# Transposing the normed attention output by DMA instead of by TensorE, in a two-layer graph network

## The reference, cut to what matters

```python
# x: (1250, 1024) float32; layer 0
qkv = x @ W_qkv                                   # 16 heads of 64
attn = relu(q @ k.T * SCALE)
out = attn @ v                                    # (1250, 1024)
normed = (out - mu) / sqrt(var + EPS) * gamma + beta
y_mix = normed @ W_out + b_out                    # "the output product"
h = x_normed @ W_gnn.T + b                        # the graph product, (1250, 1024)
y_gnn = A_hat @ h                                 # A_hat: normalized adjacency from 20000 edges
x = x + y_mix + y_gnn                             # then a gated feed-forward, then a second layer
```

## Time and profile before

| | |
|---|---|
| time, median of 3 runs | 2251.77 us (2248.81 to 2257.10) |
| profiled execution, its own time | 2240.85 us |
| its span | 2239.0 us |
| granted TensorE clock over the span | 0.967 |
| busy: PE, DVE, POOL, ACT | 93%, 55%, 48%, 33% |
| norm stage, first transpose to last unit | 686.4 to 790.2 us |
| counting stage | 793.4 to about 977 us |

### The profile page before, as it was taken

One profiled execution on the slowest core, in us unless ns is written; L12 is line 12 of the kernel. 1 busy time (PEld: TensorE's weight loads), 2 busy tenths in 40 slices (PEclk: granted clock), 3 DMA queues, 4 the chain that ended last, 5 costly groups with the idle time before them and its releaser, 6 DMA issues.

```text
span 2239.0 us, 41639 instructions
## 1 busy us (share of the span) xinstructions
PE 2082.3 (93%) x16528; PEld 1435.8 (64%) x16528; DVE 1226.5 (55%) x2232; ACT 749.0 (33%) x1095; POOL 1072.4 (48%) x794
## 2 busy tenths in 40 slices
PE   5979999999999999979999999999999999976997
PEld 5537456564548977734545577748877888864775
DVE  5881563555486799965534622546455534374332
ACT  4242553554464454320130512312112221052332
POOL 5457778787875400025503862044334326433554
PEclk8989999999999999979999999999999999987999
DMA  3311232331545321060001021201000100386886
GB/s 139 74 43 38 69 82 63 86 93 42 129 127 126 129 70 39 1 209 19 20 0 50 25 74 36 87 29 58 29 28 28 47 1 31 117 324 186 154 152 107
DMA packets 106983, 176.89 MB, mean 79 GB/s; under 512 B 31058, under 2 KB 76249, under 8 KB 100543
## 3 DMA queue, kind: packets, MB, share of 16 engines
q1 hardware_dynamic: 89966, 145.63, 20.7%
q0 software_dynamic: 16848, 28.90, 7.7%
HBM read 120.82 MB, written 53.49 MB: 78 GB/s over the span
## 4 chain that ended last, share of the span: by engine, by line
PE 82%; DVE 8%; issue 3%; POOL 2%; ACT 2%; DMA 2%; DVEq 0%; POOLq 0%; SPq 0%; ACTq 0%
PE ps L487 20%; PE ps L490 20%; PE ps L489 20%; PE pt L703 5%; PE ps L687 3%; DVE RB L784 2%; PE pt L472 2%; PE pt L881 1%; PE pt L687 1%; PE pt L1113 1%; PE ps L1132 1%; PE ps L1133 1%; PE ps L1134 1%; DVE RB L1767 1%; PE ps L1164 1%
## 5 line engine op out<-in xcount | busy, mean ns | idle before, releaser
L487 PE MATMUL ps<-WR,RB 128*128 128x256 f16 (+2 forms) x2280 | 640.4, 281 | 8.3 <-DVE SR L1767 2.9
L489 PE MATMUL ps<-WR,RB 128*128 128x256 f16 (+2 forms) x2280 | 639.7, 281 | 0.0
L490 PE MATMUL ps<-WR,RB 128*128 128x256 f16 (+2 forms) x2280 | 639.7, 281 | 0.0
L487 PEld LDWEIGHTS ps<-WR,RB 128*128 128x128 f16 x2280 | 223.8, 98 | 54.8 <-issue 4.4
L487 PE MATMUL ps<-RB,WR 128*128 128x512 f16 (+1 forms) x720 | 246.5, 342 | 9.7 <-DVE RB L439 7.4
L490 PEld LDWEIGHTS ps<-WR,RB 128*128 128x128 f16 x2280 | 223.6, 98 | 43.4 <-issue 0.8
L489 PEld LDWEIGHTS ps<-WR,RB 128*128 128x128 f16 x2280 | 224.1, 98 | 40.8 <-issue 0.6
L490 PE MATMUL ps<-RB,WR 128*128 128x512 f16 (+1 forms) x720 | 246.4, 342 | 0.0
L489 PE MATMUL ps<-RB,WR 128*128 128x512 f16 (+1 forms) x720 | 246.4, 342 | 0.0
L1423 POOL TENSOR_TENSOR WR<-WR,units 128x3072 f32<-128x3072 f32 (+2 forms) x18 | 81.4, 4521 | 339.8 <-PE ps L487 334.7
L1490 POOL DMA_INDIRECT edges_sorted<-SR x160 | 189.3, 1183 | 72.1 <-issue 55.5
(11 more groups left out here) (341 smaller groups left out, 4000.4 us busy)
## 6 DMA issues: line engine op xcount, KB each, us to landing
WR<-in_w_moe SPq DMA_DIRECT2D x64, 256.0 KB, 3.6
moe_split<-WR SPq DMA_DIRECT2D x128, 128.0 KB, 1.8
RB<-moe_split SPq DMA_DIRECT2D x8, 2048.0 KB, 13.4
WR<-in_w_mix SPq DMA_DIRECT2D x12, 1024.0 KB
WR<-in_w_mix SPq DMA_DIRECT2D x8, 1536.0 KB
RB<-in_x SPq DMA_DIRECT2D x18, 512.0 KB, 5.9
WR<-in_w_out SPq DMA_DIRECT2D x8, 1024.0 KB
RB<-counts SPq DMA_DIRECT2D x10, 640.0 KB, 4.9
```

The source lines that it names most:

```text
L487: m = nc.tensor.matmul(o, ah, bh, start=(k == 0), stop=False)
L489: nc.tensor.matmul(o, ah, bl, start=False, stop=False)
L490: m = nc.tensor.matmul(o, al, bh, start=False, stop=(k == n - 1))
```

## The change

High and low half of the normed tile are made in SBUF, row by row, in the unused tails `ozh` and `ozl` of the weight buffers: ScalarE's copy reads `z`, VectorE's subtraction reads `z` and `ozh`. Two DMA transposes on SP's queue, one for each half, write the operands `OT0h` and `OT0l`. TensorE transposes nothing in this stage, and PSUM holds nothing of it. ScalarE norms tile i+2 only when the low half of tile i is made (`oz_lo`), and reuses a half's buffer when its transpose has landed (`oz_turned`). The output product's first ten units wait for `oz_turned`. SP loads the tile's rows of `x` behind the two transposes.

```diff
-TURNS = [("ln0", NT), ("lnO", NT), ("agg0", 2 * NT), ...
+TURNS = [("ln0", NT), ("agg0", 2 * NT), ...
...
+        ozh, ozl = [w[:, 2048:3072] for w in wh], [w[:, 2048:3072] for w in wl]
...
@@ tensor
-            r0 = TURN0["lnO"]
-            for i in range(NT):
-                for u in range(max(2, 4 * i), 4 * i + 4):
-                    g_unit(pe, u)
-                pe.wait_ge(z_ready, Z0["lnO"] + i + 1)
-                pe.wait_ge(turn_lo, r0 + i - 1)
-                turn8(i % 2)
+            for u in range(2, 4 * NT):
+                g_unit(pe, u)
             T0 = TILE0["mix0_out"]
-            pe.wait_ge(turn_lo, r0 + NT)
             pe.wait_ge(evac, T0)
...
                 if st in OUTS_AT:
                     u = OUTS_AT.index(st)
+                    if u < NT:
+                        pe.wait_ge(oz_turned[u % 2], 32 * (u // 2) + 32)
@@ scalar
-                act.wait_ge(turn_done, r0 + i + 1)
-                nc.scalar.activation(nodes_of(OT0h, i), turn_view(i % 2), ACT.Copy, scale=OS0).then_inc(turn_hi, 1)
+                act.wait_ge(z_ready, Z0["lnO"] + i + 1)
+                if i >= 2:
+                    act.wait_ge(oz_turned[i % 2], 32 * (i // 2))
+                nc.scalar.activation(ozh[i % 2], z[i % 2][:, 0:DIM], ACT.Copy, scale=OS0).then_inc(oz_hi, 1)
                 if i + 2 < NT:
+                    act.wait_ge(oz_lo, i + 1)
                     norm(i + 2)
@@ sync
-                sp.wait_ge(turn_done, TURN0["lnO"] + i + 1)
+                sp.wait_ge(oz_lo, i + 1)
+                for half, o in ((ozh, OT0h), (ozl, OT0l)):
+                    sp.dma_start_transpose(out=o[:, :, i * TN:(i + 1) * TN], in_=half[i % 2]).then_inc(oz_turned[i % 2], 16)
                 sp.dma_start(X[0:rows_of(i), i], x_rows(i)).then_inc(xr_loaded[i], 16)
@@ vector
-                turn_lows(dve, "lnO", i, i % 2, OT0h, OT0l, OS0)
+                dve.wait_ge(oz_hi, i + 1)
+                stt(ozl[i % 2], zz, OS0, ozh[i % 2], ALU.mult, ALU.subtract).then_inc(oz_lo, 1)
...
+            dve.wait_ge(oz_lo, NT)
             for half in ohd[1:]:
```

More of the change, by code:

```diff
@@ L59 @@
 UP = [(0, 0), (1, 0), (0, 1), (0, 2), (1, 1), (1, 2), (2, 0), (2, 1), (2, 2)]
-TURNS = [("ln0", NT), ("lnO", NT), ("agg0", 2 * NT), ("ln1", NT), ("ln2", NT), ("gnn1", NT), ("tO", NT), ("ln3", NT)]
+TURNS = [("ln0", NT), ("agg0", 2 * NT), ("ln1", NT), ("ln2", NT), ("gnn1", NT), ("tO", NT), ("ln3", NT)]
 def firsts(table):
@@ L74 @@
 Z0 = firsts([(n, NT) for n in ("ln0", "lnO", "agg0", "ln1", "ln2", "ln3")])
-H0 = firsts([(n, NT) for n in ("ln0", "lnO", "ln1", "ln2", "gnn1", "tO", "ln3")])
+H0 = firsts([(n, NT) for n in ("ln0", "ln1", "ln2", "gnn1", "tO", "ln3")])
 class Chain:
@@ L318, in build_program @@
         turn_lo = sem("turn_lo")
+        oz_hi, oz_lo, oz_turned = sem("oz_hi"), sem("oz_lo"), [sem("oz_turned0"), sem("oz_turned1")]
         dve_chain, act_chain, pool_chain = sem("dve_chain"), sem("act_chain"), sem("pool_chain")
```

## The result

The changed kernel takes 2260.5 us at the median of eight runs (2257.30 to 2262.76), the kernel before 2251.97 us (2248.81 to 2257.10). The ratio is 1.0038, with a 95% interval from 1.0029 to 1.0047: 8.5 us slower, where 4.1 us faster were forecast. That is inside the stated range and inside the half per cent, but on the other side of it, and the interval excludes a gain.

A forecast was written before the change was run, and what follows sets the result against it. TensorE was taken to bound the norm and counting stages. 8.3 us saved, less 1.1 us for the later low half and 3.1 us for two transposes, gave 4.1 us faster, 2247.7 us; range 2240 to 2300 us.

The forecast's parts named there:

- what is added on the engines: Norm stage: ScalarE's copy 1.057 us in place of 1.013, VectorE's low half 1.193 in place of 1.220; together nothing.
- can be caught by POOL: VectorE's low half, reading SBUF alone, may be held up by POOL as `g_low` is; idle time covers it once or twice.
- the new wait of ScalarE for `oz_lo` also costs nothing: Norm stage: ScalarE already waits for POOL's `nbias` until 704.24, just when VectorE ends the low half; no cost.
- I count no stall, at most 1 to 2 us: Norm stage: VectorE lets TensorE run faster without holding it up, or for 1 to 2 us at most.
- The three units' lead: Norm stage: a lead of 7.9 us covers VectorE being held up for 4.02 us when POOL works on weights.
- -8.3 us: TensorE, norm stage: last unit ends 8.3 us earlier, from nine transpose groups of 0.87 us and 0.5 us for the first.
- The queue: DMA queue, norm stage: 47 us busy plus twenty transposes of 1.5 us is 77 us, under the stage's 105; hidden mid-stage.
- T: Queue time of one 256 KB DMA transpose: taken as 1.5 us, the lower bound; upper bound 11.3 us.
- the second rival: SP's queue in the norm stage becomes the bound once T exceeds 2.9 us, making the kernel slower; chance 0.27.
- the prediction's 10.5 us for a half: DMA transpose of one half, estimated from the skill page's 1309 ns per 128x128 tile held eight times over.
- The joint: Norm stage to counting stage: `in_w_out` load 4.2 us later, delaying row copy 3, TensorE's step 6 and what follows.
- a late hand-over eats the gain: T between 1.5 and 3.5 us, or VectorE stalls of 1 to 2 us; end -2 to +10 us; chance 0.13.

The follow-up runs named there:

- e1: Changed kernel with VectorE's statistics of tile i+2 moved from the pass's end to behind its second g_sum; 2249.5 us, ratio 0.9992 to the kernel before.
- e5: Changed kernel with one operand of VectorE's low half read from PSUM (stale scores times 0), TensorE waiting for the last low half; 2236.1 us against 2240.3, ratio 0.9983.
- e10: The early-statistics version of the changed kernel (e1) measured again, on the same chip as e9; ratio 0.9985 to the kernel before.
- e7: Changed kernel with early statistics and without the DMA transposes of tiles 1 to 9; 2235.6 us, ratio 0.9984 to the kernel before.
- e6: Changed kernel with early statistics and the second-slot load of in_w_out ahead of tile 9's transposes; 2235.1 us against 2240.3, ratio 0.9978.
- e2: Changed kernel without the DMA transposes of tiles 1 to 9, the output product reading tile 0's columns; 2258.2 us, ratio 1.0030 to the kernel before.
- e9: The changed kernel measured again, unedited, on one chip with two other repeat runs; ratio 1.0039 to the kernel before.
- e3: Changed kernel with the second-slot load of in_w_out issued ahead of tile 9's two transposes and load of x; 2259.9 us, ratio 1.0033 to the kernel before.
- e8: Changed kernel with early statistics and the load of in_w_out issued ahead of tile 9's saves of g too; 2236.5 us, ratio 0.9985 to the kernel before.

## Why the prediction was wrong

The step that failed is the one on what is added on the engines. It had the new low half cost "nothing", because its duration is the same (1.193 forecast, 1.219 measured), and saw only one direction of the collision: that VectorE "can be caught by POOL". What happened is the other direction. VectorE itself loses nothing by its operation; POOL's two small operations grow from 0.74 us together to 2.2 us. The new low half holds up `veps`, and `rstd`, now late, runs into the addition of beta, which had both operands in SBUF before the change too and met no small operation of POOL then. In the same step, "the new wait of ScalarE for `oz_lo` also costs nothing" was true by the letter: the wait for `nbias` covered it. But that wait, 1.29 us, was taken as given, and it grew to 3.17. The row was used as cover without asking whether the change would move the cover's own end. e1 takes the collision away by order, e5 by operand, and both gain 11 to 12 us; the cause is shown. Without the collision the changed kernel is 1.8 to 5.2 us faster than the kernel before at the medians (e1, e10, e5, e7, e6), around the 4.1 us that were forecast.

The Trainium skill states the rule, and it was not used. "SBUF — State Buffer", Who interferes with whom, says that a VectorE instruction with both inputs in SBUF contends with POOL's reads of SBUF, and that one with at most one SBUF input (outside of the two-port modes) does not. It calls the contention an exclusive lock, and says of the two-port modes that whoever issues first holds the shared ports for its whole instruction while the other is blocked. The trace agrees, and shows it for two SBUF inputs: `veps` is issued 0.09 us behind the low half and ends 0.05 us behind it, and with one operand in PSUM (e5) it takes its usual 188 ns.

"I count no stall, at most 1 to 2 us" failed with it. The three units' lead was to cover the one wait of 4.02 us; it does not cover that wait and the late `nbias` together. Each of the four stalls costs a little more than its idle time. In steady work a matmul starts 0.11 us after the one before it; behind a stall the idle time counts only from the end of the last matmul, 0.27 us after its start. So 8.5 us of idle time put the work off by 9.2 us. One stall costs more still, by the windows of the changed kernel (length, busy PE, granted clock, DMA share, GB/s):

```profile
735.00:738.00 3.00, 0.12 (x2) 1.00 0.00 0
738.00:742.00 4.00, 3.90 (x21) 0.57 0.37 116
```

Behind 2.98 us without work TensorE is granted 0.57 of its clock over 4 us, mostly its 1.2 GHz level. From 738.44 to 741.96 it starts 17 matmuls, which take 1.85 us at full clock: 1.7 us more.

"-8.3 us" at the end of the last unit was summed from one group too many. The group of tile 9 is the tenth, and it runs behind the last unit, not ahead of it:

```profile
790.00 1.04 PE L472 MATMUL pt<-ident,SR 128*128 128x128 f32 x8
```

Up to that end eight groups at full clock and the first one go, 8 x 0.87 + 0.5 = 7.5 us; the last 0.87 us belong to the joint, where TensorE waited for VectorE anyway. So 105.05 - 7.5 + 9.2 + 1.7 = 108.5 us are accounted for of the 108.65. The term itself was had in full. In e6, e7 and e10, with one stall of 1.05 us (1.2 us by the count above), 6.3 us should be left, and their last unit ends 6.2, 6.4 and 6.0 us earlier than before the change, counted from the first addition of beta. The 1.2 us from there to the 5 us of the left column lie between the last unit and the clearing of `Bc`: 1.8 us before the change, 3.0 in e6 and e7. This part rests on reading profiles, not on an experiment.

The queue: right in its main point, in part by wrong numbers. T was put at 1.5 us, 3 us with the fixed part, and 3.4 was measured. Over the same 120 us of the norm stage, the queue's share is 66.1% in the changed kernel and 46.2% in e2, which has sixteen transposes fewer there: 1.5 us of the queue for each. But the queue of before is busy for 45.9% of 675 to 795 us, 55 us and not the 47 us of the prediction, which read a share of 155 us as one of 120; the second rival's limit was T = 2.5 us and not 2.9. Neither the range's upper end nor the prediction's 10.5 us for a half is supported: a half of eight blocks lands in 3.1 us at best and 3.4 at the median (4.4 in e6). SP's hold, 1.3 us each, was put at half of that. It cost the stage nothing visible, but it counts at the joint.

The joint: near in sum in one profile (4.7 against 4.2 us; 2.3 us in e9), only partly in cause. L602 did wait for the load, 4.17 us, 3.25 in e9. The load's issue comes 8.7 us behind the last unit in place of 2.7: 6.0 us more where 4.2 were forecast, of which SP's hold by two transposes is 2.7 us. The load then takes 5.9 us up to L602 in place of 7.3, so that the sum came near is in part luck. And with the load early (e3, e6, e8) the right column stays at 190 us and doesn't return to 187.3; of the versions with the new low half only e7 has 187.4, and e2, also without the transposes, 188.4. Part of what is left shows in the clock, here the first 20 us from the clearing on. In order the kernel before, the changed one, e6 and e7:

```profile
792.00:802.00 10.00, 8.25 (x69) 1.00 0.53 173
802.00:812.00 10.00, 9.88 (x85) 1.00 0.31 105
```

```profile
806.80:816.80 10.00, 8.68 (x62) 0.83 0.91 264
816.80:826.80 10.00, 6.58 (x44) 0.83 0.08 27
```

```profile
786.90:796.90 10.00, 7.20 (x47) 0.77 1.08 248
796.90:806.90 10.00, 10.00 (x79) 0.89 0.17 52
```

```profile
786.10:796.10 10.00, 7.20 (x62) 1.00 0.48 171
796.10:806.10 10.00, 10.00 (x88) 1.00 0.33 106
```

154 matmuls before the change, 106 after it, 126 in e6, 150 in e7. e6 and e7 have the same busy time, but e6 has clock 0.77 and 0.89 and e7 has 1.00. The DMA share differs too (1.08 and 0.48), but it doesn't decide by itself: the first 10 us of e9, with transposes, and of e2, without them, have it the other way round.

```profile
809.70:819.70 10.00, 7.20 (x62) 1.00 0.95 280
```

```profile
808.70:818.70 10.00, 7.19 (x49) 0.83 0.49 171
```

Why the clock fell in the one and not in the other stays open. As e6 and e7 do not differ in their medians, the 2 us are at the limit of what the runs can tell.

The rivals: the third, "a late hand-over eats the gain", had the size (up to +10 us), but from T and from stalls on VectorE of 1 to 2 us. The mechanism that decided, POOL held up by VectorE, was in none of them.

## What to carry to other kernels

When an operand moves from PSUM to SBUF, look at who else uses SBUF beside it. The instruction's own duration may hardly change (1.22 us before and after here), and a small operation of POOL that starts just behind it can take as long as it does (1.18 us in place of 0.19). Look in the timeline of before for POOL instructions that start within that instruction's time, and follow what waits for them. The cure was cheap here: POOL's inputs were made ready earlier in the pass (e1).

A wait that hides a cost is only cover if the change doesn't lengthen it as well.

## What the runs showed of the hardware that was not expected

A DMA transpose of a 128x1024 float16 tile from SBUF to SBUF holds SP for 1.25 to 1.33 us at the least and at the median, longer when a large load is ahead of it, and lands in 3.1 us at best. Beside some 17 MB of other traffic, twenty of them in place of two cost the norm stage nothing that shows (e6 and e7, 101.9 and 101.7 us).

Two POOL operations on one element per partition grew from 188 and 555 ns to 981 and 1195 ns on the mean, without any change to themselves, when VectorE instructions of 1.22 us with both operands in SBUF ran beside them, and were back at 188 and 555 ns when one operand of the first of these came from PSUM (e5).
